# Attention scores from two float32r parts in two row halves instead of three bf16 parts

## The reference

```python
# layer 0, attention: 16 heads of 8 dimensions, causal
scores = einsum('bshi,bthi->bsth', q, k); masked with -inf above the diagonal, / sqrt(128)
wv = einsum('bsth,bthi->bshi', softmax(scores, axis=2), v);  x += wv @ Wo
# layer 0, feed forward: 8 experts, two chosen for each token (silu(gate) * up, down)
# layer 1, attention: RMS norm, 16 query heads over 4 key and value heads, not causal
qkt = einsum('brkqa,bkca->brkqc', q * rf, k * rf) / sqrt(128)     # rf: a table by position
s = einsum('brkqc,bkca->brkqa', softmax(qkt), v);  x += s + s @ w_o
# layer 1, feed forward: 128 -> 512 -> 128 with a sine in the middle
```

## Time and profile before

| | |
|---|---|
| median of 3 runs | 2203.51 us (2200.15 to 2205.18) |
| span of the profiled execution | 2193.3 us |
| around the span (median less span) | 10.2 us |
| TensorE, VectorE, ScalarE busy | 2032.1, 1464.8, 1189.7 us |
| attention of layer 0, of layer 1 | 116.5 to 640 us, 1302 to 2078 us |

### The profile page before, as it was taken

How to read it: one execution, slowest core, us unless ns; L and a number is a source line. 1 busy time by engine, 2 the same in 40 slices (tenths; PEclk the granted TensorE clock), 3 DMA queues, 4 the chain that set the end, 5 groups by cost and what they waited for, 6 DMA issues and landing times. The chain is left out here.

```text
span 2193.3 us, 38142 instructions
## 1 busy us (share of the span) xinstructions
PE 2032.1 (93%) x11744; PEld 893.1 (41%) x11744; DVE 1464.8 (67%) x2435; ACT 1189.7 (54%) x2374; POOL 142.6 (7%) x216
## 2 busy tenths in 40 slices
PE   4599899999999999999999789999999999999876
PEld 2244344344435666666665212222222222222355
DVE  5677577577744545455554988887886887886186
ACT  2256466466672222222322337776776777777776
POOL 3100000000000000000000100000000000000065
PEclk9689899799999999999998869999998999999998
DMA  7533324143100000000000411011111111100000
GB/s 205 129 43 38 48 27 51 28 50 41 12 2 1 0 0 0 0 0 0 0 0 1 115 15 16 16 16 17 18 26 17 16 15 16 16 2 1 1 15 24
DMA packets 75282, 56.82 MB, mean 26 GB/s; under 512 B 43120, under 2 KB 57328, under 8 KB 75120
## 3 DMA queue, kind: packets, MB, share of 16 engines
q1 hardware_dynamic: 64416, 38.62, 12.0%
q0 software_dynamic: 3072, 10.23, 1.4%
q10 hardware_dynamic: 7632, 5.88, 1.0%
HBM read 38.65 MB, written 12.32 MB: 23 GB/s over the span
## 5 line engine op out<-in xcount | busy, mean ns | idle before, releaser
L1152 DVE TENSOR_REDUCE rowmax<-ps 128x1 f32<-128x1024 f32 (+7 forms) x1024 | 971.3, 987 | 288.3 <-PE ps L571 140.0
L921 ACT ACTIVATE probs<-ps 128x512 f32<-128x512 f32 (+3 forms) x1792 | 860.2, 558 | 367.8 <-PE ps L604 217.1
L604 PE MATMUL ps<-Q,K 75*128 75x512 bf16 (+3 forms) x1792 | 547.5, 366 | 32.6 <-ACT probs L921 16.8
L571 PE MATMUL ps<-K,Q 72*128 72x512 bf16 (+3 forms) x1792 | 545.6, 380 | 34.7 <-DVE rowmax L1152 31.0
L620 PE MATMUL ps<-probs,V 128*9 128x512 f32 (+3 forms) x3584 | 450.2, 561 | 0.0
L604 PEld LDWEIGHTS ps<-Q,K 75*128 75x128 bf16 x1792 | 167.3, 99 | 398.7 <-ACT probs L921 281.3
L957 ACT ACTIVATE Q<-ps 128x512 f32<-128x512 f32 (+1 forms) x192 | 114.4, 596 | 324.5 <-PE ps L730 314.0
L571 PEld LDWEIGHTS ps<-K,Q 72*128 72x128 bf16 x1792 | 152.5, 100 | 326.4 <-DVE rowmax L1152 188.9
L1266 DVE TENSOR_TENSOR Q<-ps,Q 128x512 f32<-128x512 f32 (+1 forms) x192 | 130.2, 688 | 136.6 <-PE ps L733 136.4
L733 PE MATMUL ps<-Q,wu 128*128 (+3 forms) x384 | 197.2, 595 | 1.6 <-DVE Q L1266 1.6
L730 PE MATMUL ps<-Q,wg 128*128 (+3 forms) x384 | 196.9, 594 | 1.0 <-DVE attn L1177 1.0
(11 more groups left out here) (157 smaller groups left out, 1132.0 us busy)
## 6 DMA issues: line engine op xcount, KB each, us to landing
Q<-q_parts SPq DMA_DIRECT2D x288, 64.0 KB
K<-k_parts SPq DMA_DIRECT2D x144, 64.0 KB
q_parts<-Q POOLq DMA_DIRECT2D x16, 384.0 KB, 3.4
k_parts<-Q POOLq DMA_DIRECT2D x8, 384.0 KB, 7.6
V<-v SPq DMA_DIRECT2D x16, 144.0 KB
K<-k_parts SPq DMA_DIRECT2D x144, 16.0 KB
x<-in_L_attn_h_dram SPq DMA_DIRECT2D x4, 512.0 KB, 9.7
out_dram<-y SPq DMA_DIRECT2D x8, 256.0 KB, 2.3
```

Of the source, the lines that this page charges most:

```text
L571: last = pe.matmul(buf[:, c:e], Q[0:CROSS, slot, j, i * P:(i + 1) * P], K[0:CROSS, slot, kj, c:e], start=True, stop=not diag)
L604: last = pe.matmul(ps[:, bank, c:HALF], K[0:KROWS, q, kj, t * P:(t + 1) * P], Q[0:KROWS, q, j, h * HALF + c:(h + 1) * HALF], start=True, s ...
L921: act.activation(probs[:, (4 * m + j) % PR, c:HALF], ps[:, B_BANKS[(4 * m + j) % 3], c:HALF], ACT.Exp, scale=SCALE).then_inc(sl["exp_done" ...
L1152: dve.tensor_reduce(rowmax[:, par, 8 * j + i:8 * j + i + 1], score_a(i % 2)[:, 0:hd.keys(i)], AX, ALU.max).then_inc(sl["max_done"], 1)
```

## The change

[...] The middle part and its two operations go. Four pairs of parts make 32 rows, one row of zeros is added (CROSS = 33), and two rows for the parts of the maximum (KROWS = 35). Since four heads of 4-byte rows don't fit side by side, heads 0 and 2 of a quad lie on partitions 0 to 34, heads 1 and 3 on partitions 64 to 98 (LANE = 64). Passes A and B are float32r matmuls over 33 or 35 rows of one half. The causal mask is cut in two halves of 64 rows as well, and takes two bf16 matmuls in the half of its head. The maxima take two VectorE operations instead of four, a float32 transpose, and two DMAs instead of one. A quad's loads are 16 of 64 KB instead of 18, and the parts are written as 512 KB instead of 384 KB in each DMA. Two DMAs per slot copy the zero row into Q, once in each layer, and eight put it into K at the start. The order of letters stays as it is.

```diff
-SPL = 3
-CROSS = SPL * SPL * HD
+SPL = 2
+ROWS = SPL * SPL * HD
+CROSS = ROWS + 1
 KROWS = CROSS + SPL
+LANE = 64
...
-        Q = sb("Q", [P, SLOTS, 4, S], BF16)
-        K = sb("K", [P, SLOTS, 4, S], BF16)
+        Q = nc.alloc_sbuf_tensor_at("Q", [P, SLOTS, 2, S], F32R, offset=q_at)
+        K = nc.alloc_sbuf_tensor_at("K", [P, SLOTS, 2, S], F32R, offset=k_at)
...
+        def lane(j, rows):
+
+            return slice(LANE * (j % 2), LANE * (j % 2) + rows)
...
-                    for a in range(SPL):
-
-                        heads = q_parts[l][a, :, bass.ts(b, S)].rearrange("(h i) n -> i h n", i=HD)
-                        heads = heads[:, 4 * q:4 * q + 4, :] if l == 0 else heads[:, q:H:KV, :]
-                        for r in range(SPL):
-                            row = (a * SPL + r) * HD
-                            sp.dma_start(Q[row:row + HD, q, :, :], heads).then_inc(loaded[l][q], 16)
+                    for par in range(2 if first else 0):
+                        row = LANE * par + ROWS
+                        sp.dma_start(flat(Q, q, q + 1)[row:row + 1, :], flat(K, q, q + 1)[row:row + 1, :])\
+                            .then_inc(loaded[l][q], 16)
+                    for par in range(2):
+                        for a in range(SPL):
+
+                            heads = q_parts[l][a, :, bass.ts(b, S)].rearrange("(h i) n -> i h n", i=HD)
+                            heads = heads[:, 4 * q + par:4 * q + 4:2, :] if l == 0 else heads[:, q + KV * par:H:2 * KV, :]
+                            for r in range(SPL):
+                                row = LANE * par + (a * SPL + r) * HD
+                                sp.dma_start(Q[row:row + HD, q, :, :].bitcast(F32), heads).then_inc(loaded[l][q], 16)
...
-                    sp.dma_start(Q[CROSS:KROWS, q, :, :].rearrange("c j (i n) -> c (j i) n", n=P),
-                                 negmaxT[:, :]).then_inc(sl["negmax_rows"], 16)
+                    for par in range(2):
+                        rows = Q[LANE * par + CROSS:LANE * par + KROWS, q, :, :].bitcast(F32)
+                        sp.dma_start(rows.rearrange("c j (i n) -> c (j i) n", n=P),
+                                     negmaxT[32 * par:32 * par + 32, :]).then_inc(sl["negmax_rows"], 16)
...
-                        last = pe.matmul(buf[:, c:e], Q[0:CROSS, slot, j, i * P:(i + 1) * P],
-                                         K[0:CROSS, slot, kj, c:e], start=True, stop=not diag)
+                        last = pe.matmul(buf[:, c:e], Q[lane(j, CROSS), slot, j // 2, i * P:(i + 1) * P],
+                                         K[lane(j, CROSS), slot, kj, c:e], start=True, stop=not diag)
                         if diag:
-                            last = pe.matmul(buf[:, w - P:w], identb[:, :], causal[:, :],
-                                             start=False, stop=True)
+                            for part in range(2):
+                                last = pe.matmul(buf[:, w - P:w], identb[lane(j, LANE), part, :],
+                                                 causal[lane(j, LANE), part, :], start=False, stop=part == 1)
...
-                    last = pe.matmul(ps[:, bank, c:HALF], K[0:KROWS, q, kj, t * P:(t + 1) * P],
-                                     Q[0:KROWS, q, j, h * HALF + c:(h + 1) * HALF], start=True, stop=not diag)
+                    last = pe.matmul(ps[:, bank, c:HALF], K[lane(j, KROWS), q, kj, t * P:(t + 1) * P],
+                                     Q[lane(j, KROWS), q, j // 2, h * HALF + c:(h + 1) * HALF],
+                                     start=True, stop=not diag)
                     if diag:
-                        last = pe.matmul(ps[:, bank, c:c + P], causal[:, :], identb[:, :],
-                                         start=False, stop=True)
+                        for part in range(2):
+                            last = pe.matmul(ps[:, bank, c:c + P], causal[lane(j, LANE), part, :],
+                                             identb[lane(j, LANE), part, :], start=False, stop=part == 1)
...
-                    pe.transpose(ps[0:SPL * 32, bank, 0:P // 2].bitcast(BF16),
-                                 negmax[:, :, :].rearrange("p c n -> p (c n)"), identb[:, :])\
+                    pe.transpose(ps[:, bank, 0:P], negmax_w[:, :], ident[:, :])\
...
-                        act.activation(parts[0:r, half, n, 0, :], src, ACT.Copy).then_inc(sl["hi_done"], 1)
+                        act.activation(parts[0:r, half, n, 0, :].bitcast(F32R), src, ACT.Copy)\
+                            .then_inc(sl["hi_done"], 1)
...
-                    for n in range(2):
-                        r = rows[n]
-                        act.wait_ge(sl["rest_done"], 2 * u + n + 1 + AT_ONE)
-                        act.activation(parts[0:r, half, n, 1, :], rest[0:r, n, :], ACT.Copy)\
-                            .then_inc(sl["mid_done"], 1)
...
-                        dve.tensor_tensor(rest[0:rows[n], n, :], src[n], parts[0:rows[n], half, n, 0, :], ALU.subtract)\
-                            .then_inc(sl["rest_done"], 1)
-                    for n in range(2):
-                        dve.wait_ge(sl["mid_done"], 2 * u + n + 1)
-                        dve.tensor_tensor(parts[0:rows[n], half, n, 2, :], rest[0:rows[n], n, :],
-                                          parts[0:rows[n], half, n, 1, :], ALU.subtract).then_inc(sl["split_done"], 1)
+                        dve.tensor_tensor(parts[0:rows[n], half, n, 1, :], src[n], parts[0:rows[n], half, n, 0, :],
+                                          ALU.subtract).then_inc(sl["split_done"], 1)
...
-                    own.done(dve.tensor_scalar(negmax[:, 0, :], mx, -1.0, None, ALU.mult))
-                    own.done(dve.scalar_tensor_tensor(negrest[:, :], mx, -1.0, negmax[:, 0, :],
-                                                      ALU.mult, ALU.subtract))
-                    own.done(dve.tensor_copy(negmax[:, 1, :], negrest[:, :]))
-                    dve.tensor_tensor(negmax[:, 2, :], negrest[:, :], negmax[:, 1, :], ALU.subtract)\
-                        .then_inc(sl["negmax_ready"], 1)
+                    own.done(dve.tensor_scalar(negmax[:, :, 0, :].bitcast(F32R), mx, -1.0, None, ALU.mult))
+                    dve.scalar_tensor_tensor(negmax[:, :, 1, :], mx, -1.0, negmax[:, :, 0, :],
+                                             ALU.mult, ALU.subtract).then_inc(sl["negmax_ready"], 1)
```

More of the change, by code:

```diff
@@ L19 @@
 F32 = mybir.dt.float32
+F32R = mybir.dt.float32r
 BF16 = mybir.dt.bfloat16
@@ L168, in build @@
     out_dram = out.rearrange("b (t p) d -> p (b t) d", p=P)
+    q_at, k_at = (nc.bump_sbuf(SLOTS * 2 * S * 4)[0] for _ in range(2))
     with ExitStack() as ctx:
@@ L201, in build @@
         ident = sb("ident", [P, P])
-        identb = sb("identb", [P, P], BF16)
-        causal = sb("causal", [P, P], BF16)
+        identb = sb("identb", [P, 2, P], BF16)
+        causal = sb("causal", [P, 2, P], BF16)
         wqvk = sb("wqvk", [P, 3 * D])
@@ L242, in build @@
         qk32 = probs[:, 0:2, :]
-        rest = probs[:, 2:4, :]
-        parts = spare[:, B * S:B * S + 2 * SPL * GW].bitcast(BF16)\
-            .rearrange("p (two a c n) -> p two a c n", two=2, a=2, c=SPL)
+        parts = spare[:, B * S:B * S + 4 * SPL * GW].rearrange("p (two a c n) -> p two a c n", two=2, a=2, c=SPL)
         ew = sb("ew", [P, T, E])
@@ L265, in build, with column @@
         ps = ctx.enter_context(nc.psum_tensor("ps", [P, 8, 512], F32))
+        def column(j, i):
+            return 16 * (j % 2) + 8 * (j // 2) + i
+        def lane(j, rows):
+            return slice(LANE * (j % 2), LANE * (j % 2) + rows)
         def score_a(n):
@@ L363, in _ @@
                 for q in range(2):
-                    load(0, q)
+                    load(0, q, first=True)
                 sp.wait_ge(sl["v_taken"], NG + AT_ONE)
@@ L368, in _, with batch @@
                     sp.wait_ge(sl["parts_written"][half], 32 * (NG // 2))
-                load(0, 2)
+                load(0, 2, first=True)
                 negmax_rows(0, 0)
-                def batch(b, final):
+                def batch(b, final, fresh=False):
                     for q in range(4):
@@ L376, in batch @@
                             sp.wait_ge(sl["o_turned"], 2 * g + AT_ONE)
-                            load(b if q == 0 else b + 1, (q + 3) % 4)
+                            load(b if q == 0 else b + 1, (q + 3) % 4, first=q == 0 and fresh)
                         if q < 3 or not final:
                             negmax_rows((q + 1) % 4, g + 1)
-                with sp.Fori(0, B - 1) as b:
-                    batch(b, False)
+                batch(0, False, fresh=True)
+                with sp.Fori(0, B - 2) as b:
+                    batch(b + 1, False)
                 batch(B - 1, True)
@@ L399, in _ @@
             own.done(pool.memset(power_b[:, :], -0.5))
-            for m in (ident, identb):
```

(16 more changed lines are left out.)

83 lines of the change are left out of this document (46 added, 37 removed).

## The result

The changed kernel takes **3020.91 us** (median of 4 runs, 2987.78 to 3044.72) where the kernel before, on the same chip, takes 2202.79 (2200.15 to 2205.18). The ratio is 1.359, 95% interval 1.352 to 1.366; it rests on the two faster runs of the changed kernel, 2987.78 and 3001.11, while the profiled execution (span 3038.8 us) is one of the two slower, so that some 46 us of what the profile shows are not in the ratio. Forecast were 2137 us, with 2085 to 2275 as the range. The change makes the kernel a third slower.

A forecast was written before the change was run, and what follows sets the result against it. The prediction took TensorE's stream to set the pace inside the attention quads. Its terms, -84 + 20 - 6 + 0 + 3 = -67, took 2203.5 us to a forecast of 2137 us, range 2085 to 2275.

The forecast's parts named there:

- formula: TensorE's matmul time: columns / 2.4 GHz plus 2.5 ns, fitted to the steps of both layers' attention.
- Part 1: Price of a float32r matmul: one pass for 256 columns and more; 0.112 us for 128 columns (bounds 0.056, 0.223).
- Part 2: Layer 1's attention: matmuls of different row halves overlap, a quad goes from 47.8 to 42.2 us, in all -84 us.
- Rival (a): Attention: row halves don't overlap, layer 1 gains nothing and layer 0 pays; 2268 us in all, chance 0.22.
- rival (c): Layer 1's attention: halves overlap but engines wait for one another, quad 44 us or more; 2164 in all, chance 0.10.
- Part 3: Layer 0's attention: doubled masks and 128-column float32r matmuls make a quad 33.84 us against 32.49, in all +20 us.
- two-lane walk: TensorE's written order with two halves running at once, without waits: 39.6 us a quad in layer 1, 31.85 in layer 0.
- Rival (b): Layer 0's attention: halves overlap, but 128-column float32r matmuls cost four passes, +47 in place of +20; 2164 us, chance 0.17.
- Part 4: Projection: the middle part's operations go, layer 1's groups take 4.2 us instead of 4.80, -6 us; layer 0's projection 0.
- Part 5: Small things: negmax and its DMAs 0, masks ahead of layer 0's first quad +2, fills and pad transfers at most +1.

The follow-up runs named there:

- e2: The kernel before (bf16, one lane) with pass A over rows 0 to 32 and pass B over 0 to 34, most cross terms left out: 3292.0 us.
- e1: The changed kernel with passes A and B over all 64 rows of their half, the added rows zeros in K: 2350.26 us, ratio 1.069 to before.
- e3: e1 with passes A and B over all 128 rows, both halves at once, masks still 64 rows in one half: 2849.93 us.
- e7: e3 with each causal mask as one matmul over 128 rows in place of two over 64: 2355.69 us.
- e9: e1 with row maxima over at most 256 keys and exponentials over at most 256 columns, TensorE's work whole: 2274.24 us.
- e8: e5 with row maxima over at most 256 keys and exponentials over at most 256 columns, TensorE's work whole: 2021.82 us.
- e4: The changed kernel with all matmuls of passes A and B and all masks in the lower half, so nothing overlaps: 3466.73 us.
- e10: e5 with all matmuls of passes A and B and all masks in the lower half, so no two overlap: 2368.97 us.
- e5: The changed kernel with three bf16 parts, six products in 64 rows of each half, and the projection of before: 2156.66 us, ratio 0.981 to before.

## Why the prediction was wrong

**The step that failed** is one that it never wrote down as a step: the columns of every matmul were priced at the rate of the full clock (the 2.4 GHz of its formula is fitted to starts 0.215 us apart) because the granted clock of before was 1.00 ("In both the granted clock is 1.00") and TensorE stayed 99% busy. The change cuts the rows of a matmul from 72 and 75 to 33 and 35, and with them the clock went from 1.00 to 0.50 in the quads of layer 1, and in eleven of layer 0's fifteen to between 0.50 and 0.56. In layer 1 it did not come back from the low stretch ahead of the first quad until the last one. e2 shows it on the old kernel, e1 undoes it on the new one. It doubles layer 1's stream and nearly doubles layer 0's, and is some 690 of the profile's 845 us (3038.8 against e1's 2351.0; nearer 740 if e1's late start is taken off; by the medians 671 of 818). Busy records alone don't tell the clock: layer 1's quad has 78.76 of 79.10 us busy at 0.50, the one of before 47.24 of 47.80 at 1.00.

**Part 1, price of float32r.** The forecast sums over one pass for 256 columns and more, a choice between two bounds that no row of before settled. The runs then showed one pass: at 512 columns 0.427 us at half clock and 0.224 to 0.236 at full clock (e3, layer 1), and at 256 columns 0.121 to 0.122 to the mask in five of the eight such places of e7's quad from 210.9 us, where four passes would take 0.43 (0.204 to 0.227 in the other three, which I read as an open load). "For 512 columns the load lies behind the stream" was wrong: float32r costs TensorE 3.5 us a quad in layer 1 and 4.0 in layer 0 (e9 less e8), and in layer 1 most of it sits in starts 0.11 later than the columns explain, which I read as loads left open behind a V step or a wait. The 128-column price was 0.112; in the same quad of e7 it is 0.062 to 0.065 in five places and 0.146 to 0.167 in three, which I read as the load hidden and open.

**Part 2, row halves.** They overlap as walked: matmuls start 3 ns apart, quads of 79.1 = 2 x 39.6, and 41.4 at full clock with light neighbours (e8). Rival (a) is refuted by e4 and e10; e10, with bf16, has the 47.9 us that (a) gave layer 1's quad. Of the forecast 5.6 us a quad bf16 gets 2.1 (e5) and float32r none (49.0 against 47.8). The waits of 1.5 that the prediction added for the engines were too small: 4.3 (e5 less e8). That is rival (c)'s "44 or more", at 45.7, and it had 0.10.

**Part 3, masks.** Forecast 33.84 us. At full clock e5 has 33.4 and e1 36.7; bf16's +0.9 a quad over the 32.49 is twice what the two-lane walk gives it (31.85 + 1.1 - 32.49 = 0.46), and e1's other 3.3 are float32r. So at full clock the change would have paid 4.2 a quad here, not 1.35: the forecast's +20 is +63 by e1. Rival (b), four passes for 128 columns, is refuted by the starts in e7.

**Part 4, projection.** Layer 1's, VectorE's timeline after, against the earlier trace rows:

```profile
1579.67 1.28 DVE L1147 TENSOR_TENSOR probs<-ps,ropeT 128x512 f32<-128x512 f32 x2
...
1583.75 1.28 DVE L1147 TENSOR_TENSOR probs<-ps,ropeT 128x512 f32<-128x512 f32 x2
...
1588.11 1.28 DVE L1147 TENSOR_TENSOR probs<-ps,ropeT 128x512 f32<-128x512 f32 x2
```

4.1 and 4.4 us a group against 4.80, as forecast (4.2); the last three groups take longer, and from the first to the last start of a product with the rotary table the stage takes 35.0 us against 38.1: -3, not -6. Layer 0's ends 8 us sooner (last copy of V at 72.4, before 80.1), but so does e5's (69.8), which has the old projection; I can't put that down to the change.

**Part 5** was too small to see. **The range** could not hold: its upper end was rival (a) at full clock.

**Still open:** how many rows are enough, why rows count at all, and why 64 in one lane hold a full clock but regain it so late, wasn't measured; nor which of buffers and order makes the 4.3 us between engines.

## What to carry to other kernels

A change that narrows the contraction of the matmuls that fill TensorE can halve the clock, however full the queue looks (e2, with 33 and 35 rows in place of 72 and 75: 0.50 in place of 1.00 with TensorE busy for all of the 88.20 us): before pricing columns, compare the rows of each matmul with those of the matmuls that had the clock of 1.00, and give "the clock falls" a chance of its own. Padding with zero rows was a cheap cure here (e1: 3021 to 2350 us with not one column less). Float32r cost 3.5 and 4.0 us a quad (e9 less e8), 0.12 at the two matmuls shown ahead of a V step (0.65 us in e1 against 0.53 in e5), which their 512 columns didn't hide; keeping bf16 and taking the row halves alone (e5) gave 1.9%, of the 3% that the forecast promised.

## What the hardware showed that I had not expected

- TensorE 99% busy at a granted clock of 0.50 for over a millisecond in the changed kernel (1148.15 of 1163.10 us), and 100% busy at 0.50 in quads of 88.2 and 91.9 us with 33 and 35 rows in one lane (e2 bf16, e4 float32r); 1.00 in the quads shown with 64 rows in each half, though 13 or more of them are zeros (e1, e5).
- 64 rows in one half alone: 1.00 in the quad of 47.9 us, but 88.3 us fully busy at 0.50 before it (e10).
- Matmuls that alternate between 128 rows and 64 lose some 0.2 us per pair of changes, and with it much of the clock: 0.64 against 1.00, and 75.1 against 37.2 us a quad (e3, e7). The lost clock costs far more than the 0.2 us. The changed kernel has no such changes at its masks; e3 brought them in.
